# Seven block products for the second unit, with expert 0's weight sums made beside the first unit's outputs

## The chip, the core and the metric

The kernel runs on one core of one Trainium2 chip. The metric is the device time of one execution in microseconds (us). The engines are PE (TensorE matmul), ACT (ScalarE), DVE (VectorE), POOL (GpSimd) and SP (SyncE, which here only issues DMAs). Each engine works through its own instructions in order, and they meet only at semaphores.

## The reference

```python
h = layernorm(x) * (1 + ca) + sa                 # x: 4 x 2048 x 512
x = x + ga * attn(h)                             # rmsnorm, one 512 -> 1536 product, gated scan over time
h = layernorm(x) * (1 + cb) + sb
probs = softmax(h @ Wr); topk_probs, topk_experts = top_k(probs, 2)     # 8 experts
buf[e, b, pos] += h                              # at most 320 tokens per expert and batch row, the rest dropped
h1 = relu(buf @ W1 + b1)                         # 512 -> 2048
y  = h1 @ W2 + b2                                # 2048 -> 512
out = x + gb * sum over the 2 chosen experts of prob * y[token]
```

## The kernel before

The 8192 tokens are worked through in 16 blocks of 512 (four per batch row). An attention part runs over the blocks; each block is then normed, routed and its rows scattered by POOL into a table of slots in HBM (two times four indirect DMAs, line 710). The route of a block is route_choose (14 linked small DVE operations, line 1246), positions (a few small matmuls, line 1802) and route_place (up to 14 more links, line 1267). The last blocks, 14 and 15, are routed inside the first expert unit.

The expert part has 16 units, v = 0 to 15: expert e = v // 2 and half u = v % 2. A unit is 640 slots (two batch rows of 320). Every float32 factor is split into a high and a low float16 part, so each product is three matmuls. First layer: 512 to 2048 for 640 slots. Second layer: five column tiles of 128 slots, each 48 matmuls of 512 columns, in two PSUM banks by turns; column tile t needs the first operation of outputs(t - 2) (line 1446), which empties its bank.

Units below PLAIN (here 2) are plain: 16 column blocks hb of 24 matmuls of 320 columns, for two batch rows each. ACT and DVE follow in 32 steps i = 2 hb and 2 hb + 1: ACT makes the relu twice (float32 and float16) and DVE subtracts for the low part. Because b is the innermost loop, both steps of an hb end together. A step may be at most four ahead of the next engine's. Between the steps stand the last blocks' pieces, by hand: last_block(i) on DVE (line 1463) and ACT (line 906), last_block(hb) on PE (line 1864) behind the matmuls of hb, so that PE stands still there if its condition is not met. DVE also takes the maxima of w2 of expert 0 at steps 14, 16, 18 and 20, makes its scale at step 21 (w_scale, which goes over POOL's all_max) and the low parts (w_lo) at 25, 27, 29 and 31; ACT casts the high parts at 24, 26, 28 and 30.

Other units use seven block products in place of eight (Strassen's scheme in Winograd's form), 336 matmuls for 384, in a pipeline written out by slots: eight column pairs p, each started PERIOD = 7 slots after the one before, with pair_step(v, p, k) on PE, ACT and DVE for slot k = t - 7 p. They need sums of the four blocks of W1 (sums, line 1576, four linked DVE operations for each of two halves f, then ACT's casts sums_hi and DVE's rests sums_lo) and of the inputs (x_sums and x_lo, line 1597). For expert e + 1 this is made beside the outputs of unit (e, 1), after its weights were read once for their maxima (max_piece, line 1491) and loaded again.

Weights pass through four staging quarters q in reg_d. On SP, bring() waits until a quarter was released (s_rel[q], counted) and issues a 512 KB load (line 563), which counts s_fill[q]. fill_max, fill_w1 and fill_w2 give the number of loads ahead of a purpose. The order of SP's queue is that of experts() (line 591). Unit 1's input load (load_unit, a DMA transpose, line 538) waits for all scatters.

## Time and profile before

| | us |
|---|---|
| median of 3 runs | 2186.25 |
| lowest, highest | 2185.34, 2189.82 |
| profiled execution, its own time | 2185.74 |
| span of its profile | 2184.0 |
| PE busy | 2149.5 |
| DVE busy | 1602.7 |
| ACT busy | 1030.6 |

The span is what the profile shows from the first to the last instruction; times in rows are counted from its start. A PE matmul's busy time overlaps the next one's, so lengths of stretches are taken from starts. "Idle before" in a row is how long the engine stood still ahead of it, and the arrow names what released it.

### The profile page before, as it was taken

How to read it: one execution, taken by the hardware profiler on the slowest of the kernel's cores; microseconds unless marked ns; L12 is line 12 of the kernel's file. 1: busy time of each engine (PE TensorE's matmuls, PEld its weight loads, DVE VectorE, ACT ScalarE, POOL GpSimd, SP SyncE). 2: the span in 40 equal slices, each digit the busy share in tenths (PEclk: the TensorE clock that was granted, in tenths of full speed). 3: DMA queues.
4: the chain of work that ended last, by engine and by line, in shares of the span. 5: the costliest groups of instructions: out<-in, count | busy, mean ns of one | idle time of the engine just before them, and what ended most of it. 6: DMA issues, size and time to landing. Idle time of an engine off the chain costs nothing.

```text
span 2184.0 us, 33604 instructions
## 1 busy us (share of the span) xinstructions
PE 2149.5 (98%) x12538; PEld 1185.8 (54%) x12538; DVE 1602.7 (73%) x2850; ACT 1030.6 (47%) x2042; POOL 365.5 (17%) x334
## 2 busy tenths in 40 slices
PE   7999999999999999999999999999999999999997
PEld 2444454545564656556464655556464655656463
DVE  6799999999883587587668758775975887587341
ACT  5466666766370545246153625534461544356050
POOL 1124343343423010100101010110101010000101
PEclk9999999999999999999999999999999999999999
DMA  7799996775675344344534534452445345343301
GB/s 275 243 245 254 239 246 159 184 175 125 159 207 129 102 121 142 86 112 116 136 88 121 144 89 123 109 150 70 104 139 120 94 129 150 78 102 97 44 6 25
DMA packets 350883, 296.73 MB, mean 136 GB/s; under 512 B 242331, under 2 KB 242331, under 8 KB 350208
## 3 DMA queue, kind: packets, MB, share of 16 engines
q1 hardware_dynamic: 328960, 252.44, 41.5%
q0 software_dynamic: 21760, 42.14, 10.3%
q8 instruction: 99, 1.62, 0.3%
q14 instruction: 64, 0.52, 0.1%
HBM read 159.64 MB, written 93.01 MB: 116 GB/s over the span
## 4 chain that ended last, share of the span: by engine, by line
PE 90%; DVE 5%; SPq 1%; issue 1%; DMA 1%; ACT 1%; POOL 0%; DVEq 0%; ACTq 0%; POOLq 0%
PE bank L1979 36%; PE bank L1915 29%; PE bank L1831 20%; PE bank L1903 3%; PE bank L1786 1%; DMA reg_e<-reg_e 1%; SPq L491 0%; SPq L473 0%; PE bank L1742 0%; DVE reg_a L1568 0%; DVE reg_c L1179 0%; DVE reg_b L1438 0%; DVE mxw L1157 0%; DMA mod_rows<-reg_a 0%; PE bank L1797 0%
## 5 line engine op out<-in xcount | busy, mean ns | idle before, releaser
L1979 PE MATMUL bank<-reg_b,reg_c 128*128 128x512 f16 x3840 | 834.2, 379 | 1.2 <-DVE reg_b L1438 1.0
L1979 PEld LDWEIGHTS bank<-reg_b,reg_c 128*128 128x128 f16 x3840 | 375.3, 98 | 450.4 <-DVE reg_e L1456 2.1
L1831 PE MATMUL bank<-reg_c 128*128 128x512 f16 x2304 | 507.1, 379 | 1.5 <-DMA reg_c<-reg_a 1.4
L1915 PE MATMUL bank<-reg_e,reg_a 128*128 128x320 f16 x2688 | 417.7, 299 | 0.0
L1831 PEld LDWEIGHTS bank<-reg_c 128*128 128x128 f16 x2304 | 222.8, 98 | 260.7 <-issue 2.7
L1915 PEld LDWEIGHTS bank<-reg_e,reg_a 128*128 128x128 f16 x2688 | 262.2, 98 | 105.2
L736 POOL DMA_INDIRECT out_dram<-reg_e,midx x80 | 139.5, 1744 | 1007.2 <-DVE reg_e L1460 898.6
L1456 DVE SCALAR_TENSOR_TENSOR reg_e<-bank,inv,reg_e 128x512 f32<-128x512 f32 x80 | 59.8, 748 | 255.9 <-PE bank L1979 255.9
L947 ACT ACTIVATE reg_e<-bank,b1s 128x320 f32<-128x320 f32 x112 | 59.1, 527 | 390.4 <-PE bank L1915 390.4
L1915 PE MATMUL bank<-reg_e,reg_d 128*128 128x320 f16 x1344 | 217.0, 299 | 0.0
L1915 PEld LDWEIGHTS bank<-reg_e,reg_d 128*128 128x128 f16 x1344 | 130.4, 98 | 53.8 <-ACT reg_e L947 3.8
L689 POOL DMA_INDIRECT slot_rows<-reg_e,sli x112 | 129.2, 1154 | 100.7 <-DVE reg_e L1295 65.7
L1495 DVE TENSOR_REDUCE wm<-reg_d 128x1 f32<-128x1024 f32 x112 | 132.6, 1210 | 0.0
L1011 ACT ACTIVATE reg_e<-reg_e 128x2560 f16<-128x2560 f32 x14 | 32.7, 2337 | 194.3 <-DVE reg_e L1615 194.3
L1550 DVE SCALAR_TENSOR_TENSOR reg_e<-bank,reg_e 128x320 f32<-128x320 f32 x112 | 55.0, 491 | 85.3 <-PE bank L1915 84.2
L1915 PE MATMUL bank<-reg_e 128*128 128x320 f16 x672 | 109.6, 299 | 0.0
L1903 PE MATMUL bank<-reg_e,reg_a 128*128 128x320 f16 x768 | 105.9, 299 | 1.4 <-ACT reg_c L931 1.3
L856 ACT ACTIVATE reg_e<-bank,iq 128x512 f32<-128x512 f32 x60 | 40.9, 681 | 135.0 <-PE bank L1831 127.8
L1903 PEld LDWEIGHTS bank<-reg_e,reg_a 128*128 128x128 f16 x768 | 74.7, 98 | 31.3 <-ACT reg_c L931 2.3
L975 ACT ACTIVATE reg_c<-reg_e 128x320 f16<-128x320 f32 x112 | 52.1, 465 | 66.5 <-DVE reg_e L1550 66.5
L1568 DVE SCALAR_TENSOR_TENSOR reg_a<-reg_d,wsc,reg_a 128x1024 f16<-128x1024 f32 x56 | 69.4, 1281 | 16.8 <-ACT reg_a L989 16.8
L1915 PEld LDWEIGHTS bank<-reg_e 128*128 128x128 f16 x672 | 65.8, 98 | 27.8
(231 smaller groups left out, 2597.3 us busy)
## 6 DMA issues: line engine op xcount, KB each, us to landing
reg_d<-in_w SPq DMA_DIRECT2D x224, 512.0 KB, 4.1
slot_rows<-zrow SPq DMA_DIRECT2D x32, 516.0 KB, 5.1
reg_b<-in_x SPq DMA_DIRECT2D x16, 1024.0 KB, 7.6
out_dram<-reg_b SPq DMA_DIRECT2D x16, 1024.0 KB, 6.9
reg_d<-in_w SPq DMA_DIRECT2D x8, 1024.0 KB, 10.0
slot_rows<-zrow SPq DMA_DIRECT2D x32, 129.0 KB, 4.8
reg_d<-in_wmod SPq DMA_DIRECT2D x4, 1024.0 KB, 14.5
reg_e<-mod_rows SPq DMA_DIRECT2D x7, 512.0 KB, 4.1
```

The source lines that it names most:

```text
L689: g.indirect_dma_start(out=rows, out_offset=bass.IndirectOffsetOnAxis(ap=sli[:, pj % 2, k, t:t + 1], axis=0), in_=rowi[:, pj % 2, t, :], i ...
L736: g.indirect_dma_start(out=out, out_offset=bass.IndirectOffsetOnAxis(ap=midx[:, u, t:t + 1], axis=0), in_=yo[:, i % 2, :], in_offset=None, ...
L947: a.activation(part_of[:, n % 2, :], u_bank, ACT.Identity, bias=ba[:, p:p + 1], scale=HID_SHIFT).then_inc(s_r0, 1)
L975: a.activation(hid[:, 0, p, CAP:UNIT], part_of[:, 2 + n % 3, :], ACT.Relu).then_inc(s_h12, 1)
L1456: v_.scalar_tensor_tensor(yv[:, i % 2, :], bank_y[i % 2][:, :], inv2[:, u, kind:kind + 1], b2t, ALU.mult, ALU.add).then_inc(s_yd, 1)
L1495: v_.tensor_reduce(wm[:, which, k:k + 1], stage_q[:, q, :, :].rearrange("p c h -> p (c h)"), AX, ALU.max, apply_absolute_value=True).then_ ...
L1550: v_.scalar_tensor_tensor(part_of[:, 2 + n % 3, :], bank_v[n % 2][:, 0:CAP], HID_SHIFT, part_of[:, 2 + n % 3, :], ALU.mult, ALU.add).then_ ...
L1568: v_.scalar_tensor_tensor(lo, stage_q[:, q, :, :], wsc[:, 0:1], hi, ALU.mult, ALU.subtract).then_inc(s, 1)
L1831: ins = mm(dst[:, :], wqs[:, ws, kc, e0:e0 + P], xns[:, j % 2, xs, kc, :], start=kc == 0 and xs == 0 and ws == 0, stop=kc == KC - 1 and ws ...
L1903: ins = mm(bank_h[i % 4][:, 0:CAP], w1s[ws][:, kc, hb * P:(hb + 1) * P], xT_of(u)[:, 4 * xs + kc, b * CAP:(b + 1) * CAP], start=kc == 0 an ...
L1915: ins = mm(dst[:, 0:CAP], w[ws][:, c, p * P:(p + 1) * P], xs_of[:, KC * xs + 2 * i + c, j * CAP:(j + 1) * CAP], start=first and c == 0 and ...
L1979: ins = mm(bank_y[i % 2][:, :], hid[:, hs, hc, t * P:(t + 1) * P], w2s[:, ws, hc, :], start=k == 0 and hs == 0 and ws == 0, stop=k == HC - ...
```

## The change

PLAIN becomes 1: unit 1 has seven products too. For it, W1 of expert 0 is loaded again by quarters behind w_lo, in two halves (the second behind unit 1's input load on SP's queue), and DVE and ACT make its sums, their casts and rests, and the sums of unit 1's inputs, beside unit 0's outputs. Expert 1's first maxima for W1 move: four pieces to unit 0's outputs(3), four into the first four periods of unit 1, its scale_head to slot 30 and scale_tail to slot 51 there; the pieces for W2 stay in unit 1, eight, at slot 5 of each period. POOL's all_max(1, 0) moves in front of unit 1's outputs. In unit 0, block 15's norm (apply2, row_hi, lo2) moves ahead of block 14's routing, block 14's routing moves later (PE's logits from hb 2 to 4, positions from 5 to 6; DVE's route_choose from step 5 to 10, route_place from 9 to 14), and block 15's moves earlier (route_choose from 22 to 21, positions from hb 13 to 12, route_place from 28 to 25).

```diff
@@ constants
-PLAIN = 2
-W2_NEXT = 6
+PLAIN = 1
+W1_NEXT_HEAD, W1_NEXT_TAIL = 30, 51
@@ fill_max, fill_w1, fill_w2
-            return 8 * (e - 1) + 2 * which
+            return 8 * e - 6 + 2 * which
-            return 8 * (e - 1) + 4
+            return 8 * e - 2 if e else 0
-            return 8 * (e - 1) + 6
+            return 8 * e
@@ SP, experts()
-                bring_w1(1, fill_max(1, 0), 0)
+                bring_w1(0, fill_w1(0), 0)
                 for k in range(2):
                     sp.wait_ge(s_send[k], 16 * 2 * TB * NB // 2)
                 sp.wait_ge(s_xt, 16)
                 load_unit(1, 1)
+                bring_w1(0, fill_w1(0), 1)
+                bring_w1(1, fill_max(1, 0), 0)
@@ POOL
+                    if e == 0 and u == 1:
+                        all_max(1, 0)
-                        if e + 1 < E and u == 0 and t == (2 if e else 3):
+                        if 0 < e and e + 1 < E and u == 0 and t == 2:
@@ ACT, last_block(i)
+                if i in (7, 8):
+                    row_hi(n, 2 * (i - 7), 2 * (i - 7) + 2)
-                if i == 6:
+                if i == 12:
                     exps(n - 1)
-                if i in (10, 11):
-                    row_hi(n, 2 * (i - 10), 2 * (i - 10) + 2)
-                if i == 23:
+                if i == 22:
                     exps(n)
@@ ACT, sums_hi(e, f)
+                if e == 0:
+                    act.wait_ge(s_wlo, 8)
+                    act.wait_ge(s_mm1, 2 * HC)
                 for k, (w, q) in enumerate(((w_s1, 3), (w_s3, 2), (w_s2, 0), (w_s4, 1))):
-                    wait(act, s_ssum, 4 * (2 * (e - 1) + f) + k + 1)
+                    wait(act, s_ssum, 4 * (2 * e + f) + k + 1)
+                    if e == 0 and k == 3:
+                        for m in range(2):
+                            act.wait_ge(s_send[m], 16 * 2 * TB * NB // 2)
@@ ACT, behind unit 0
+                    if v == 0:
+                        sums_hi(0, 0)
                     if PLAIN <= v + 1 < 2 * E:
                         x_hi(v + 1)
+                    if v == 0:
+                        sums_hi(0, 1)
@@ DVE, last_block(i)
                 if i == 3:
                     apply2(q, j, 0)
-                if i == 5:
+                if i == 6:
+                    apply2(q, j, 1)
+                if i == 8:
+                    lo2(n, j)
+                if i == 10:
                     route_choose(q, j - 1)
-                if i == 7:
-                    apply2(q, j, 1)
-                if i == 9:
+                if i == 14:
                     route_place(q, j - 1)
-                if i == 11:
-                    lo2(n, j)
-                if i == 22:
+                if i == 21:
                     route_choose(q, j)
-                if i == 28:
+                if i == 25:
                     route_place(q, j)
@@ DVE, plain_unit(u)
-                    elif i >= W2_NEXT and i % 3 == 0 and (i - W2_NEXT) // 3 < 8:
-                        max_piece(1, 1, (i - W2_NEXT) // 3)
@@ DVE, pairs(v), u == 1
-                        if t % PERIOD == 2 and 1 <= t // PERIOD <= 8:
+                        if t % PERIOD == (2 if e else 5) and 1 <= t // PERIOD <= 8:
                             max_piece(e + 1, 1, t // PERIOD - 1)
+                        if e == 0 and t % PERIOD == 0 and 1 <= t // PERIOD <= 4:
+                            max_piece(1, 0, 3 + t // PERIOD)
+                        if e == 0 and t == W1_NEXT_HEAD:
+                            scale_head(1, 0)
+                        if e == 0 and t == W1_NEXT_TAIL:
+                            scale_tail(1, 0)
@@ DVE, beside_outputs(e, u, t), u == 0 and e == 0
                     if t == 0:
+                        sums(0, 0)
+                        sums_lo(0, 0)
+                    if t == 1:
+                        x_sums(1)
+                        sums(0, 1)
+                    if t == 2:
+                        x_lo(1)
+                        sums_lo(0, 1)
+                    if t == 3:
                         for k in range(4):
                             max_piece(1, 0, k)
-                    if t == 3:
-                        for k in range(4, 8):
-                            max_piece(1, 0, k)
-                        scale_head(1, 0)
-                    if t == 4:
-                        scale_tail(1, 0)
@@ PE, last_block(hb)
-                if hb == 2:
+                if hb == 4:
                     ... logits of block 14
-                if hb == 5:
+                if hb == 6:
                     positions(NB - 2, B - 1, BPB - 2)
-                if hb == 13:
+                if hb == 12:
                     positions(NB - 1, B - 1, BPB - 1)
@@ PE, pair_step, P1
-                    if p % 4 == 0 and v % 2 == 0:
+                    if p % 4 == 0 and (v % 2 == 0 or v == 1):
```

## Rows read from the trace of the kernel before

**Rows 1.** The page, part 1: busy us (share of the span) xinstructions.

```profile
PE 2149.5 (98%) x12538; PEld 1185.8 (54%) x12538; DVE 1602.7 (73%) x2850; ACT 1030.6 (47%) x2042; POOL 365.5 (17%) x334
```

**Rows 2.** Busy time by stretch: us, then PE, PEld, DVE, ACT, POOL, clock, DMA share.

```profile
589.50:648.30 58.80, 56.56 (x476) 40.97 (x475) 49.66 (x115) 38.91 (x82) 14.95 (x16) 1.00 0.75 194
701.50:753.70 52.20, 52.20 (x386) 37.57 (x384) 25.37 (x43) 26.83 (x61) 1.55 (x1) 1.00 0.29 86
753.70:805.50 51.80, 51.80 (x243) 23.49 (x241) 43.76 (x49) 19.45 (x19) 7.07 (x5) 1.00 0.50 111
805.50:903.00 97.50, 97.50 (x579) 56.21 (x577) 61.85 (x102) 38.98 (x73) 9.90 (x6) 1.00 0.48 125
```

**Rows 3.** Timeline of PE, end of unit 0: start, us, engine, operation, idle before.

```profile
629.43 0.25 PE L1797 MATMUL bank<-wrs,reg_e 128*128 128x16 f16 x4
...
630.23 9.94 PE L1903 MATMUL bank<-reg_e,reg_a 128*128 128x320 f16 x72
...
641.57 6.86 PE L1903 MATMUL bank<-reg_e,reg_a 128*128 128x320 f16 x47 [1.14 <-ACT reg_c L931]
648.27 5.34 PE L1979 MATMUL bank<-reg_b,reg_c 128*128 128x512 f16 x24
...
657.36 44.19 PE L1979 MATMUL bank<-reg_b,reg_c 128*128 128x512 f16 x204 [0.31 <-DVE reg_b L1438]
```

**Rows 4.** Timeline of DVE in unit 0.

```profile
596.80 0.49 DVE L1628 TENSOR_TENSOR reg_c<-reg_e,reg_c 128x320 f16<-128x320 f32 x1 [2.35 <-ACT reg_c L931]
...
605.82 0.18 DVE L1253 COPY lgs<-bank 128x32 f32<-128x32 f32 x1
...
608.73 0.19 DVE L1266 TENSOR_TENSOR mh<-oh 128x32 f16<-128x32 f32 x1
...
648.19 0.18 DVE L1273 TENSOR_TENSOR eqt<-bank,lim 128x32 f32<-128x32 f32 x1
...
651.81 2.35 DVE L1438 SCALAR_TENSOR_TENSOR reg_b<-reg_d,wsc,reg_b 128x2048 f16<-128x2048 f32 x1
...
654.88 2.34 DVE L1438 SCALAR_TENSOR_TENSOR reg_b<-reg_d,wsc,reg_b 128x2048 f16<-128x2048 f32 x1
```

**Rows 5.** Timeline of ACT in unit 0.

```profile
595.82 0.53 ACT L930 ACTIVATE reg_e<-bank,b1s 128x320 f32<-128x320 f32 x1 [8.50 <-PE bank L1786]
...
636.54 0.32 ACT L807 ACTIVATE prb<-dlg,ir 128x32 f32<-128x32 f32 x1 [1.21 <-DVE dlg L1256]
...
642.22 2.02 ACT L898 ACTIVATE reg_b<-reg_d,wsc 128x2048 f16<-128x2048 f32 x1
```

**Rows 6.** Timeline of POOL: scatter of block 15.

```profile
652.25 2.81 POOL L715 DMA_INDIRECT slot_rows<-reg_e,sli  x1 [18.05 <-DVE reg_e L1295]
655.36 2.71 POOL L715 DMA_INDIRECT slot_rows<-reg_e,sli  x1 [0.31 <-issue]
...
664.77 0.98 POOL L715 DMA_INDIRECT slot_rows<-reg_e,sli  x1 [0.30 <-issue]
```

**Rows 7.** Timeline of SP's queue: issue of unit 1's load.

```profile
666.89 6.79 SPq L538 DMA_TRANSPOSE reg_e<-slot_rows  x1
```

**Rows 8.** Line 563 on SP, 675.9 to 678: issues, time to landing.

```profile
L563 SPq DMA_DIRECT2D reg_d<-in_w x2: 578/696/813, 675.5 to 676.3; - x2
...
DMA to landing us min/median/max: 8.3/8.5/8.7
```

**Rows 9.** Tile reg_d, 700 to 760: last line, eight fills' time to landing.

```profile
DMA to landing us min/median/max: 3.3/3.5/5.2
```

**Rows 10.** Timeline of DVE in unit 3.

```profile
917.67 1.21 DVE L1495 TENSOR_REDUCE wm<-reg_d 128x1 f32<-128x1024 f32 x1
919.54 0.49 DVE L1550 SCALAR_TENSOR_TENSOR reg_e<-bank,reg_e 128x320 f32<-128x320 f32 x1 [0.66 <-PE bank L1915]
...
956.48 1.23 DVE L1583 TENSOR_TENSOR reg_d<-reg_d 128x1024 f32<-128x1024 f32 x1 [0.49 <-DVE reg_a L1568]
```

**Rows 11.** Timeline of PE in unit 3, second layer.

```profile
990.36 10.53 PE L1979 MATMUL bank<-reg_b,reg_c 128*128 128x512 f16 x48 [0.15 <-DVE reg_e L1456]
```

7 lines of the change are left out of this document (4 added, 3 removed).

## The prediction

> **What bounds the kernel now.** I read the page's busy shares first: PE is busy for 98% of the span [rows 1], so whatever adds or removes PE time near unit 1 moves the end, and idle time elsewhere only matters where PE comes to wait for it. Then the busy time by stretch [rows 2]: unit 0's first layer takes 58.8 us with 56.6 busy; unit 1 takes 52.2 for its first layer and 51.8 for its second, with PE never idle; unit 2, which has seven products, takes 97.5 in all, also without idle time. All stretches run at a granted clock of 1.00. Last come the timelines of PE, ACT, DVE, POOL and SP around unit 0, because the change takes work out of unit 1's PE stream and puts its preparation, and a new order, into unit 0. The waits PE has there now are small: 1.14 us on ACT, and in the second layer 36 matmuls take 9.1 us (648.27 to 657.36) where at the 44.19/204 = 0.217 us of the row after it they would take 7.8, so 1.3 us of waits [rows 3].
>
> **What it saves.** A plain unit has 16 x 24 = 384 matmuls of 320 columns, one with seven products 8 x 7 x 6 = 336. Units 1 and 2 differ in nothing else for PE: 52.2 + 51.8 - 97.5 = 6.5 us saved [rows 2]. One column block ("hb", 24 matmuls) of a plain unit is 52.2/16 = 3.26 us. If all the rest hid beside PE, this would be the result. So I go through what is moved.
>
> **Unit 0's first layer: the new order of block 14's and 15's routing.** PE calls positions() behind hb 6 for block 14, and waits there for the whole of route_choose, which DVE now starts at step 10 instead of 5. Steps 10 and 11 both end with hb 5. From then: ACT is free, and DVE's subtraction of step 10 starts 1.05 us later (596.80 against 595.82 for the first of ACT's two copies, and about 0.07 before it) [rows 4, 5]; it takes 0.41 (0.49 busy, 0.08 of it under the next), and route_choose 3.1 (605.82 to 608.73 + 0.19) [rows 4]. That is 4.6 us, but PE is there after 3.26: a wait of 1.3 us. Before, there were two hb blocks more between them.
> Block 15: DVE's chain now runs without a pause from step 14 to route_choose at step 21. From the end of hb 7: 1.05, route_place 3.05 (the one at 648.19 is released to POOL by 652.25, with 0.85 of start on POOL, so 3.2; block 14's has one link less), four maxima of 2048 columns at 2.2 (twice the 1.13 net of a max_piece of 1024), eight subtractions of 0.41 = 3.3, route_choose 3.1: 19.3 us [rows 4, 6, 10]. PE reaches positions() behind hb 12 after 5 x 3.26 + 0.8 (logits, 629.43 to 630.23 [rows 3]) = 17.1: a wait of 2.2. Before, route_place and lo2 of that chain lay ahead of step 14.
> The exponent chain w_scale (some 1.8 us, an estimate: five links at route_choose's 0.22 and 0.7 for POOL's part) now stands behind that route_choose. From its end PE needs 0.1 + 3.26 to reach hb 14, while ACT needs w_scale, one cast of w2 (2.0 busy, 1.9 net [rows 5]) and a pair of relus (0.8): 4.3 with the last semaphore, so about 0.9 of wait there, then 0.25 at hb 15, as each pair of steps costs ACT 1.64 + 1.9 against PE's 3.26. Waits of today that this replaces: 1.14 [rows 3] and about 0.5 unlabelled (641.57 + 47 matmuls ends before 648.27); the first comes from ACT's wait for the routing [rows 5]. Sum: 1.3 + 2.2 + 0.9 + 0.25 and 0.15 for each restart, minus 1.6, gives **+3.0 us**: the second layer starts at 651.3, not 648.27. In its first column tile PE waits for w_lo: the four end at 650.6, 653.7, 656.8 and 659.9 (route_place now stands ahead of the first; 2.26 each and one or two subtractions between), PE needs them at 651.3, 653.9, 656.5, 659.1: 0.9 of waits against 1.3 today. Net +2.6; column tile 3 can start at 651.3 + 0.9 + 3 x 10.36 = **683.3**. Bounds: 1.5 (both routing waits only half as long, from the 0.41 steps hiding in gaps) and 4.
>
> **Unit 0's second layer: the new sums.** Column tile 3 needs the first operation of outputs(1), and DVE has x_sums(1) and sums(0,1) ahead of that. sums(0,1) needs four fills; SP issues them behind unit 1's load, and this waits for all of block 15's scatter. route_place(15) follows the subtraction of step 25, and this ACT's relu behind its first cast of w2, so it runs from 645.1 to 648.3, where today's ends at 651.4: sooner by 3 us. But the scatter's eight issues on POOL are not of one length: those at 652.25 and 655.36 take 2.81 and 2.71, the last 0.98 [rows 6], and each starts inside a w_lo of DVE, an operation with two SBUF sources (651.81 and 654.88), and ends 0.85 to 0.9 after it [rows 4]. So with all four w_lo beside the scatter, four of its issues are long, not two: starts at 649.15, 651.8, 654.9, 657.95, then 661.0, and four short ones of 1.28 each (or slowed by the sums, from 662 on): the last ends at 665.9 to 666.9. Today it ends at 665.75 and SP goes on at 666.89 [rows 6, 7]. I take 667.5: **nothing of the 3 us arrives**.
> By the Trainium skill, "SBUF — State Buffer", section "Who interferes with whom", a DVE instruction with two SBUF inputs holds up only GpSimd work that reads SBUF, and it infers that descriptor generation is not held up; by that the scatter would be over by 660 and the wait below a third as long (rival B). The rows of POOL speak against it here.
> From 667.5: the load takes 6.8 of SP [rows 7], its small one 0.6, so the first fill goes out at 674.9. Today's four there, the first at 674.3 and the last at 676.3, landed up to 8.7 us after issue, at 685.0: 10.7 from first to last landing [rows 8]. Same here: 685.6. Then four sums of 1.26 (1.23 busy) [rows 10] and the 0.75 of outputs(1): 691.5. PE waits 691.5 - 683.3 = **8.2 us**. Lower bound: four fills at the 1.7 us each that they show when nothing else moves (8.8 after the first) and a send complete at 667.0: 5.9. Upper: 10, if the sums slow the scatter and are slowed by it. The first half, sums(0,0) from 662.3 and their rests until 672.1, is ready 0.1 before tile 2 wants it (672.9, with 0.75 for outputs(0)): nothing, though without room. ACT's new waits (s_wlo 8, s_mm1, s_send) have x_hi(1) and the other casts queued behind them, and these are later wanted than the fills. Tile 4 wants outputs(2) at 701.4; x_lo and four rests make it 700.8: nothing.
>
> **Unit 1's first layer: two maxima a period.** A period of seven products lasts 5.71 us (42 x 52.2/384 [rows 2]); DVE's seven operations in it at 0.41 and one max_piece at 1.13 net are 4.0, and 0.66 of the gap stands before L1550 [rows 10]. For four periods there are two. 1.13 more fits, but max_piece(1,1,k) waits for a fill that can only start when max_piece(1,0,4+k) has released the quarter, 5 slots before. Release to landing: 3.3/3.5/5.2 us [rows 9]. So one period is 1.24 + 3.5 + 0.06 + 1.13 + two subtractions 0.82 = 6.75: DVE falls back by 1.04 a period. C12 may be 1.75 us late (three products, 2.45, less its own 0.5 and the semaphores) before PE waits at P5. It is late by 1.0, 2.1 and, with the three links of scale_head at t = 30, 3.6 in the periods k = 0, 1, 2: waits 0.45 and 1.7, **2.15 us**. Bounds: 1.0 with landings of 3.3 and 4 with one of 5.2. all_max(1,0) moves on POOL in front of unit 1; nothing is queued behind it that is wanted before.
> **Unit 1's second layer.** Unit 3, the same work, has output 2 0.15 us late for PE [rows 11], so this chain has no room; the last max_piece now stands three slots later and delays C12 and all behind it by 0.6 to 1.0 us. **+0.8** (0.3 to 1.3).
>
> **Sum.** -6.5 + 2.6 + 8.2 + 2.15 + 0.8 = +7.25 us, from the profiled execution's 2185.74 (span 2184.0 and 1.7 around it), 0.5 below the median of the three runs, 2186.25. On the median: **2193.5 us**, 0.33% slower. About 0.2% (4.4 us) is what a measurement of this kernel can tell from no change.
>
> **The rivals.**
> A, all hidden: the waits I find are absorbed, by buffers that I miscounted, and today's 1.6 us of waits in the first layer go as well. 2186.25 - 6.5 - 1.6 = 2178.1. For it: unit 2 and unit 0's present order show hardly a wait. Against it: route_choose against one hb block is plain arithmetic on rows. 0.12.
> B, ends on the other side: not slower. The scatter keeps 1.28 a issue, is over at 659 and SP loads unit 1 at 660.2; the fills then wait only for the rests of the first half (671.0) and land alone by 679.9; outputs(1) at 685.8, a wait of 2.5 instead of 8.2: 2187.8. It decides when that wait is under 5.3 us, which needs the sends complete by about 664.5. For it: six of today's eight issues are short. Against: the long ones lie under w_lo. 0.20.
> C, the loop of fills in unit 1 is worse: landings of 5.0 us, as one of eight shows [rows 9], make a period 8.25, 2.5 over; three such add 4.5: 2198.0. Two loads a period share the engines, but seldom at once. 0.06.
> That seven products save nothing in unit 1 I give no chance of its own: unit 2 is the same code.
> The forecast itself has 0.62.
>
> **Chances and range.** The forecast's own bounds are -6.5 + 1.5 + 5.9 + 1.0 + 0.3 = +2.2 and +13, seldom all at one end: nine tenths of it is over 2190.6. Slower: 0.56 + 0.06 = 0.62; same: 0.06 and nearly all of B, 0.25; faster: A and a little, 0.13. The range takes in B and leaves out A and the far end: 2185 to 2199.
>
> **What would show it.** PE waits behind hb 6 and hb 12, on DVE's L1266-type link, of 1.3 and 2.2 us; four POOL issues over 2.6 us in the scatter of block 15; unit 1's load issued at about 667; one PE wait of 8 us ahead of unit 0's column tile 3, on outputs(1); in unit 1 two PE waits of 0.4 and 1.7 at P5 and DVE idle ahead of max_piece(1,1,0..3); unit 1 as a whole at 100.5 us. Wrong if the load goes out before 664 (B), or no wait shows behind hb 6 (then DVE or ACT has more room than I count).

## The result and the profile after

The changed kernel takes 2193.39 us in the median of 20 runs (lowest 2189.44), the kernel before 2186.4 beside it (20 runs, lowest 2184.81): a ratio of 1.0030, with a 95% interval of 1.0023 to 1.0037. It is 0.3% slower, as forecast (2193.5), and the forecast range holds it. One run of the changed kernel took 3237.11 us at a granted clock of 0.655, where all others have 0.99 or more, and is left out of the ratio.

The profiled execution is the fastest of those runs: 2189.44 us, span 2187.7. It has to be read as such. Unit 0 starts at 589.08 in it and at 589.53 in the kernel before, and from there to the end it takes 1600.36 us against 1596.21, 4.15 more. The medians differ by 7.0. I come back to the other 3 us.

First the page's busy shares of the changed kernel:

```profile
PE 2144.8 (98%) x12490; PEld 1180.4 (54%) x12490; DVE 1639.8 (75%) x2896; ACT 1044.0 (48%) x2051; POOL 375.8 (17%) x334
```

Then its busy time by stretch (PE, PEld, DVE, ACT, POOL, clock, DMA share); the stretches are unit 0's first layer, its second, unit 1's first, its second, and unit 2.

```profile
589.10:650.60 61.50, 56.63 (x475) 40.72 (x474) 49.35 (x127) 39.26 (x82) 16.57 (x17) 1.00 0.71 185
650.60:708.95 58.35, 53.87 (x243) 23.51 (x241) 47.47 (x44) 15.50 (x15) 21.07 (x11) 0.97 0.61 174
708.95:755.50 46.55, 45.07 (x332) 31.98 (x330) 36.98 (x74) 26.34 (x60) 3.42 (x3) 1.00 0.47 140
755.50:808.95 53.45, 52.76 (x248) 23.98 (x246) 46.50 (x54) 20.04 (x20) 7.08 (x5) 1.00 0.48 116
808.95:906.30 97.35, 97.35 (x576) 56.12 (x575) 61.91 (x102) 39.05 (x73) 9.90 (x6) 1.00 0.47 129
```

The 48 products fewer are there (12490 against 12538 in [rows 1]), and PE is busy 4.7 us less. Unit 1 takes 100.0 us instead of 104.0 [rows 2]. Unit 0 gives it back: its first layer takes 61.5 instead of 58.8, its second 58.35 instead of 53.1. And one number in the second row is new: the granted clock is 0.97. Which waits stand behind this is shown by the waits of PE, from unit 0 to the end (us in total, times, longest), and the timeline of PE in units 0 and 1:

```profile
PE bank L2001 <- DVE reg_e L1470: 4.6, 2, 3.9
PE bank L1828 <- DVE mh L1280: 3.2, 2, 2.0
PE bank L1937 <- DVE reg_e L1564: 1.5, 1, 1.5
```

```profile
616.84 0.19 PE L1828 MATMUL bank<-mh,upper 128*128 128x32 f16 x1 [1.19 <-DVE mh L1280]
639.48 0.19 PE L1828 MATMUL bank<-mh,upper 128*128 128x32 f16 x1 [1.97 <-DVE mh L1280]
...
643.93 6.86 PE L1925 MATMUL bank<-reg_e,reg_a 128*128 128x320 f16 x47 [0.76 <-ACT reg_c L935]
650.62 5.34 PE L2001 MATMUL bank<-reg_b,reg_c 128*128 128x512 f16 x24
...
659.31 23.54 PE L2001 MATMUL bank<-reg_b,reg_c 128*128 128x512 f16 x108 [0.32 <-DVE reg_b L1452]
686.74 22.37 PE L2001 MATMUL bank<-reg_b,reg_c 128*128 128x512 f16 x96 [3.89 <-DVE reg_e L1470]
...
735.11 0.99 PE L1937 MATMUL bank<-reg_e,reg_d 128*128 128x320 f16 x6 [1.48 <-DVE reg_e L1564]
...
798.60 10.53 PE L2001 MATMUL bank<-reg_b,reg_c 128*128 128x512 f16 x48 [0.69 <-DVE reg_e L1470]
```

Every wait stands where the forecast has one: behind hb 6 and hb 12 (L1828, on the last link of route_choose), at ACT's relu, ahead of column tile 3 (the row with 3.89), once at P5 of unit 1's pairs (the forecast has two there) and once at its output 2. Only the size of the one before tile 3 differs much: 3.9 instead of 8.2. These rows answer [rows 3, 11].

Why tile 3 waits: POOL's scatter of block 15, then SP's load of unit 1 (start, time that the issue takes), then DVE's work ahead of outputs(1).

```profile
648.39 2.48 POOL L717 DMA_INDIRECT slot_rows<-reg_e,sli  x1 [8.21 <-DVE reg_e L1309]
...
657.24 2.76 POOL L717 DMA_INDIRECT slot_rows<-reg_e,sli  x1 [0.30 <-issue]
660.31 0.97 POOL L717 DMA_INDIRECT slot_rows<-reg_e,sli  x1 [0.31 <-issue]
...
666.30 4.67 SPq L538 DMA_TRANSPOSE reg_e<-slot_rows  x1
...
673.29 2.83 DVE L1622 TENSOR_TENSOR reg_e<-reg_e 128x2560 f32<-128x2560 f16 x1 [0.24 <-DMA reg_e<-slot_rows]
...
681.02 1.23 DVE L1598 TENSOR_TENSOR reg_d<-reg_d 128x1024 f32<-128x1024 f32 x1 [1.46 <-DMA reg_d<-in_w]
```

The scatter starts 3.9 us sooner than in [rows 6], and the load goes out at 666.30, 0.6 before that of [rows 7]: four long issues instead of two (648.39 to 657.24) eat the gain up, as forecast. But the load then takes SP 4.67 us instead of 6.79, and the four fills behind it are used 9.4 us after the first of them is issued (671.63 to 681.02).

Of PE's 3.89 us only 1.70 are time in which DVE itself stands idle for a DMA: 0.24 ahead of the sums of x and 1.46 ahead of the second half's sums (the last two rows). DVE is busy for the rest, from its first sums at 661.81 on, with work that stands ahead of outputs(1). So an earlier load of x, or earlier fills behind it, could have taken 1.7 us off this wait and no more.

Last, what the forecast doesn't have at all, in three stretches of 4 us around the wait ahead of tile 3 (the clock is the number after POOL's):

```profile
682.00:686.00 4.00, 0.85 (x4) 0.20 (x2) 3.90 (x5) 3.45 (x3) 0.00 (x0) 1.00 0.00 0
686.00:690.00 4.00, 3.26 (x9) 1.22 (x10) 3.96 (x6) 1.15 (x1) 1.71 (x1) 0.57 0.00 0
690.00:694.00 4.00, 4.00 (x20) 1.82 (x19) 4.00 (x5) 0.00 (x0) 1.80 (x1) 1.00 0.44 49
```

Busy for 4.00 us at full clock, PE has 20 products in the last row; busy for 3.26 us behind the wait it has 9, at a mean granted clock of 0.57, nearly all of it at the lower level (1.2 GHz). The 96 products of tiles 3 and 4 take 22.37 us; at the 0.217 of [rows 3] they would take 20.8. So the wait costs 1.6 us again after it is over.

### The profile page after: what moved, and what is told of

The parts are those of the page before. It is cut to its first block, busy times and chain, and to the rows that moved or that the text cites. A ratio compares the mean times of both kernels' runs of the same rounds, so it can differ in the third digit from the quotient of the medians.

```text
span 2187.7 us, 33619 instructions
## 1 busy us (share of the span) xinstructions
PE 2144.8 (98%) x12490; PEld 1180.4 (54%) x12490; DVE 1639.8 (75%) x2896; ACT 1044.0 (48%) x2051; POOL 375.8 (17%) x334
## 4 chain that ended last, share of the span: by engine, by line
PE 86%; DVE 7%; DMA 2%; issue 2%; SPq 2%; POOL 1%; ACT 0%; DVEq 0%; POOLq 0%; ACTq 0%
PE bank L2001 33%; PE bank L1937 30%; PE bank L1853 20%; PE bank L1808 1%; DMA reg_d<-in_w 1%; DVE reg_a L1582 1%; PE bank L1925 1%; SPq L473 0%; POOL slot_rows L717 0%; DVE wmx L1393 0%; PE bank L1764 0%; DMA reg_d<-in_wmod 0%; DVE reg_e L1247 0%; DMA reg_e<-reg_e 0%; DVE reg_c L1193 0%
## 5 line engine op out<-in xcount | busy, mean ns | idle before, releaser
L1937 PE MATMUL bank<-reg_e,reg_a 128*128 128x320 f16 x2880 | 447.5, 299 | 0.0
L1937 PEld LDWEIGHTS bank<-reg_e,reg_a 128*128 128x128 f16 x2880 | 280.9, 98 | 112.7
L951 ACT ACTIVATE reg_e<-bank,b1s 128x320 f32<-128x320 f32 x120 | 63.3, 528 | 414.6 <-PE bank L1937 414.5
L1937 PE MATMUL bank<-reg_e,reg_d 128*128 128x320 f16 x1440 | 232.5, 299 | 1.5 <-DVE reg_e L1564 1.5
L1937 PEld LDWEIGHTS bank<-reg_e,reg_d 128*128 128x128 f16 x1440 | 139.5, 98 | 59.4 <-ACT reg_e L951 4.0
L691 POOL DMA_INDIRECT slot_rows<-reg_e,sli x112 | 129.7, 1158 | 100.3 <-DVE reg_e L1309 65.3
L1937 PE MATMUL bank<-reg_e 128*128 128x320 f16 x720 | 117.4, 299 | 0.0
L1937 PEld LDWEIGHTS bank<-reg_e 128*128 128x128 f16 x720 | 70.4, 98 | 29.7
L964 ACT ACTIVATE reg_e<-bank,b1s 128x320 f32<-128x320 f32 x120 | 63.4, 528 | 39.9 <-PE bank L1937 39.9
L1545 DVE SCALAR_TENSOR_TENSOR reg_c<-reg_e,reg_c 128x320 f16<-128x320 f32 x120 | 59.0, 492 | 30.4 <-ACT reg_c L960 28.9
```

Source lines behind the costliest of these rows:

```text
L691: g.indirect_dma_start(out=rows, out_offset=bass.IndirectOffsetOnAxis(ap=sli[:, pj % 2, k, t:t + 1], axis=0), in_=rowi[:, pj % 2, t, :], i ...
L951: a.activation(part_of[:, n % 2, :], u_bank, ACT.Identity, bias=ba[:, p:p + 1], scale=HID_SHIFT).then_inc(s_r0, 1)
L964: a.activation(part_of[:, 5 + n % 2, :], u_bank, ACT.Identity, bias=bb[:, NP + p:NP + p + 1], scale=HID_SHIFT).then_inc(s_r2c, 1)
L1545: v_.scalar_tensor_tensor(hid[:, 1, p, 0:CAP], part_of[:, n % 2, :], 0.0, hid[:, 0, p, 0:CAP], ALU.max, ALU.subtract).then_inc(s_l11, 1)
L1937: ins = mm(dst[:, 0:CAP], w[ws][:, c, p * P:(p + 1) * P], xs_of[:, KC * xs + 2 * i + c, j * CAP:(j + 1) * CAP], start=first and c == 0 and ...
```

## The experiments

For each run the timeline of PE gives the same marks, in us from the first product of unit 0 (that start itself lies at 589 to 596 us in these executions, in kernels that don't differ up to it). "To the end" is the profiled time minus that start. That start alone moves by 7.4 us from one execution to the next, which the medians hold and the marks don't. From unit 2 to the end every kernel takes 1380.0 to 1380.5 us, so all that differs lies ahead of it. Each row is one execution: the same first layer takes 61.5 us in five of them and 62.4 in e9. Ratios are to the kernel before on the same chip, whose median was 2187.1 beside the first four runs, 2187.6 beside the next four, 2190.6 beside three more and 2192.4 beside the last.

| kernel | layer 1 of unit 0 | layer 2 | unit 1 | unit 2 starts | to the end | ratio (95%) |
|---|---|---|---|---|---|---|
| before | 58.7 | 53.1 | 104.0 | 215.8 | 1596.2 | 1 |
| after | 61.5 | 58.3 | 100.0 | 219.9 | 1600.4 | 1.0030 (1.0023 to 1.0037) |
| e1 old order | 58.7 | 66.7 | 101.4 | 226.9 | 1607.3 | 1.0041 (1.0027 to 1.0055) |
| e2 only order | 61.5 | 52.7 | 104.0 | 218.2 | 1598.6 | 1.0013 (1.0004 to 1.0022) |
| e3 outputs first | 61.5 | 52.8 | 105.5 | 219.9 | 1600.3 | 1.0022 (1.0013 to 1.0031) |
| e4 maxima later | 61.5 | 59.9 | 99.2 | 220.6 | 1601.0 | 1.0033 (1.0021 to 1.0045) |
| e5 short w_lo | 61.5 | 57.1 | 100.1 | 218.7 | 1598.7 | 1.0012 (1.0002 to 1.0021) |
| e8 mixed order | 58.3 | 59.7 | 100.6 | 218.6 | 1599.0 | 1.0015 (1.0006 to 1.0024) |
| e6 mixed, outputs first | 58.3 | 52.8 | 106.1 | 217.2 | 1597.6 | 1.0011 (1.0002 to 1.0020) |
| e9 longer wait | 62.4 | 65.3 | 100.2 | 227.9 | 1608.0 | 1.0058 (1.0040 to 1.0076) |
| e10 before, mixed | 60.1 | 52.7 | 104.0 | 216.7 | 1597.1 | 1.0007 (0.9998 to 1.0016) |
| e7 all three | 61.0 | 53.2 | 107.9 | 222.1 | 1602.5 | 0.9998 (0.9986 to 1.0010) |
| e11 maxima spread | 63.0 | 54.3 | 104.6 | 221.9 | 1602.2 | 0.9999 (0.9987 to 1.0011) |
| e13 fills first | 60.7 | 62.2 | 102.2 | 225.1 | 1605.4 | 1.0029 (1.0017 to 1.0041) |

### What the new order costs, alone

e2 is the kernel before with the new order of blocks 14 and 15 in unit 0's first layer, and nothing else of the change.

```
 last_block of DVE                   ACT: row_hi at 7, 8; exps(n - 1) at 12; exps(n) at 22
-5 choose 14,  9 place 14            PE:  logits 14 at hb 4, positions 14 at hb 6,
-7 apply2, 11 lo2, 22 choose, 28 place    positions 15 at hb 12
+6 apply2, 8 lo2, 10 choose 14
+14 place 14, 21 choose, 25 place
```

> The kernel before with the new order of unit 0's first layer alone; unit 1 stays plain. Theory: 2.6 us slower than before (waits of 1.2 and 2.0 us at the two positions, 0.8 at hb 14, less 1.6 of today's), nothing given back, since nothing later waits for block 15's rows. Rival (the order costs nothing by itself, the waits come from the new work around it): within 0.5 us of before.

Measured: 2190.63 in the median, ratio 1.0013, and by the marks 2.3 us more than before: the +2.6 of the forecast. Its PE shows

```profile
PE bank L1806 <- DVE mh L1266: 3.2, 2, 2.0
```

at the positions, the same 1.19 and 1.97 as the changed kernel. So the order by itself is somewhat under half of the loss by the ratios (1.0013 of 1.0030), and it is paid without the seven products too.

e1 is the changed kernel with the old order put back.

> The change with the order of unit 0's first layer as it was before (logits, positions, route_choose, route_place, row_hi, exps at their old places); seven products in unit 1 stay. Theory (one chain by way of block 15's scatter, SP's load and the fills sets column tile 3): PE's waits behind hb 6 and hb 12 (1.2 and 2.0 us) go, the second layer starts some 2.5 us sooner, but route_place(15) ends 3 us later and the scatter not sooner, so the wait ahead of column tile 3 grows by as much: within 1 us of the changed kernel. Rival (the costs add up independently): 2.8 us less than the changed kernel. Second rival (the new order brings the load sooner, as it was meant to): slower by 3 us.

By the marks it takes 6.9 us more than the changed kernel. So the theory (within 1 us) fell, and the second rival came, slower because the new order brings the load sooner. The median, 2197.29, points the same way, but the ratios of the two differ by 0.0011 only and their intervals overlap.

```profile
673.09 10.53 PE L2001 MATMUL bank<-reg_b,reg_c 128*128 128x512 f16 x48 [0.68 <-DVE reg_e L1470]
...
693.18 23.84 PE L2001 MATMUL bank<-reg_b,reg_c 128*128 128x512 f16 x96 [9.56 <-DVE reg_e L1470]
```

The old order lets PE come to tile 3 some 2.8 us sooner, but unit 1's load goes out 1.2 us later (78.4 after unit 0's start, 77.2 in the changed kernel), and the fills, issued 1.5 later, are used 11.9 us after the first is issued instead of 9.4. The wait grows by what PE is early and the fills are late, and the clock is at 0.50 for longer behind it. So in the changed kernel the 2.8 us of the new order cost nothing by themselves, since PE has to wait ahead of tile 3 in any case, and the order brings the issue of the fills 1.5 us sooner. The other 2.5 us, from issue to use, aren't shown to come from the order: other kernels show 9.1 to 13.4 us there. My theory had judged it by the 0.6 us by which the load moved against the kernel before, and not by what the kernel with seven products and the old order would have.

e8 tells which part of the order pays. Block 14's steps go back, block 15's choice, placing and positions stay.

```
-DVE 6 apply2, 8 lo2, 10 choose 14, 14 place 14     ACT row_hi 7, 8; exps 14 at 12    PE hb 4, 6, 12
+DVE 5 choose 14, 7 apply2, 9 place 14, 11 lo2      ACT row_hi 10, 11; exps 14 at 6   PE hb 2, 5, 12
 DVE 21 choose 15, 25 place 15                      ACT exps 15 at 22
```

> The changed kernel, with block 14's steps in unit 0's first layer back at the places of the kernel before (apply 7, place 9, lo2 11, choose 5, row_hi 10 and 11, exps 6, logits hb 2, positions hb 5) and only block 15's choice, placing and positions at the new ones (21, 25, hb 12). Theory (the old order was slower by 3 to 4 us because block 15's placing came late there, and the new one pays 1.2 us for block 14's positions at hb 6): the wait of 1.2 at block 14's positions goes, the load is issued as in the changed kernel, about 77 us after the start of unit 0, tile 3 waits about 4: 2191.5 to 2193. Rival (block 15's norm has to come sooner, with row_hi at 7 and 8 and lo2 at 8, for its choice to be on time; the places of the choice alone bring nothing): a wait of 2 us or more ahead of block 15's positions or logits, load at 78 or later, tile 3 waits more than 6: 2195 to 2197 as in the old order.

```profile
640.59 0.18 PE L1828 MATMUL bank<-mh,upper 128*128 128x32 f16 x1
644.92 6.86 PE L1925 MATMUL bank<-reg_e,reg_a 128*128 128x320 f16 x47 [0.65 <-ACT reg_c L935]
...
667.42 4.80 SPq L538 DMA_TRANSPOSE reg_e<-slot_rows  x1
...
687.98 23.53 PE L2001 MATMUL bank<-reg_b,reg_c 128*128 128x512 f16 x96 [4.01 <-DVE reg_e L1470]
```

Not one wait is left at either positions, not only block 14's (e13, with the same order, has one of 0.73 us at block 15's): the second, 1.97 us, had also come from block 14's late steps in front of block 15's. The first layer takes 58.3 us, less than before, and the load goes out 74.1 us after unit 0's start instead of 77.2. Theory and rival both had the load at 77 us or later and missed that. It is 2190.66 in the median, below the theory's 2191.5 to 2193, and the ratio is 1.0015: about half of the loss is gone. (The wait ahead of tile 3 stays at 4.0, since PE is early by as much as the load, and the slow clock behind it takes 1.2 us more than in the changed kernel, so only 1.4 of the 3.3 us arrive by the marks.)

e10 is the kernel before with that same mixed order.

> The kernel before (unit 1 with nine products), with block 15's choice, placing and positions alone at their new places (VectorE 21 and 25, TensorE hb 12, exps at 22) and block 14 left where it was. Theory (the 2.3 us that the change's whole order costs in the kernel before come from block 14's later steps and the waits that they cause; block 15's part costs nothing): no wait ahead of either positions, first layer of unit 0 in 58.3 us against 58.74, the whole at most 0.5 below the kernel before: ratio 0.9995 to 1.0000. Rival (block 15's sooner placing pushes VectorE's remainders and the second layer's w_lo): waits of 1 us or more at the second layer's start, ratio 1.0005 to 1.001.

Neither quite. No wait at the positions, but the first layer takes 60.1 instead of 58.3, 1.2 of it a stall ahead of the logits for which the profile has no releaser; e7 and e13 show one of that size too and e11 one in three parts (0.19, 0.49, 0.56), while e6 and e8, with the same order on another chip, don't. The ratio 1.0007 (0.9998 to 1.0016) can't be told from no change. What that stall is stays open.

### What makes tile 3 wait

e5 shortens the operations of DVE that lie beside the scatter.

```
-v_.scalar_tensor_tensor(lo, stage[:, c, :], wsc[:, 1:2], hi, ALU.mult, ALU.subtract)
+v_.tensor_scalar(lo, stage[:, c, :], wsc[:, 1:2], None, ALU.mult)   # w2 of expert 0 only
```

It leaves out the subtraction of the high part, so the low part is not the remainder; the number of products is the same.

> The changed kernel, with the four low parts of expert 0's second weights (w_lo, 2.35 us each on VectorE, two SBUF sources) made by one tensor_scalar with a single SBUF source. Left out: the high part is no longer subtracted, so w2's low part of expert 0 is not the remainder; the number of products is the same. Disputed: what lengthens four of the eight issues of block 15's scatter on GpSimd (2.48 to 2.76 us instead of 0.97). Theory (an operation of VectorE with two sources in SBUF holds GpSimd's issues back): all eight issues take about 1 us, the scatter is over by some 6.5 us sooner from the start of unit 0, SyncE's transposing load of the block's x is issued about 6 us sooner (71 instead of 77.2 us after the start of unit 0), and the wait of 3.9 us ahead of unit 0's column tile 3 goes or falls below 1, with the slow clock behind it: 3 to 5.5 us less than the changed kernel, 2188 to 2190. Rival (it is VectorE's share of the SBUF as such, or the weights' traffic, whatever the operation's form): the four issues stay at 2.5 or more and the time within 1 us of 2193. Second rival (the issues get short, but the load isn't what the wait hangs on: the fills of the stage buffers are): issues short, load sooner, the wait of tile 3 still above 2.5 us.

```profile
650.05 1.60 POOL L717 DMA_INDIRECT slot_rows<-reg_e,sli  x1 [8.20 <-DVE reg_e L1309]
...
655.90 0.97 POOL L717 DMA_INDIRECT slot_rows<-reg_e,sli  x1 [0.30 <-issue]
657.18 1.61 POOL L717 DMA_INDIRECT slot_rows<-reg_e,sli  x1 [0.30 <-issue]
...
649.47 1.29 DVE L1456 TENSOR_SCALAR reg_b<-reg_d,wsc 128x2048 f16<-128x2048 f32 x1 [0.30 <-DVE reg_e L1309]
...
663.78 4.77 SPq L538 DMA_TRANSPOSE reg_e<-slot_rows  x1
...
671.66 1.28 DVE L1588 SCALAR_TENSOR_TENSOR reg_e<-reg_d,wsc,reg_e 128x1024 f16<-128x1024 f32 x1
...
686.96 22.58 PE L2007 MATMUL bank<-reg_b,reg_c 128*128 128x512 f16 x96 [2.77 <-DVE reg_e L1476]
```

Both halves of it teach something. DVE's operations take 1.28 us instead of 2.35, and still four of POOL's issues are long, 1.6 to 1.7, one under each (the fourth, with none of DVE's beside it, takes 0.97): the first ends at 651.65, 0.89 after DVE's first (650.76), where in the changed kernel the first ends at 650.87, 0.91 after its w_lo (647.61 + 2.35). So the theory's mechanism holds (DVE holds the issue until its own operation is over), but not its reason: one SBUF source is enough. Second, the load goes out 4.2 us sooner by the marks, and the wait falls by 1.1 only. The fills can't follow: the first goes out at 671.76, when the third of the first sums' remainders has freed its buffer (the row at 671.66 is the fourth; the third ends at 671.74). That is what the second rival said, and it is rival B of the forecast, whose working gave a wait of 2.5 us. But DVE is idle for only 0.68 us ahead of these sums, where it was idle for 1.70 in the changed kernel: what is left of the wait, 2.1 us, is DVE's own work from its first sums on. The ratio is 1.0012, down from 1.0030.

e9 makes the wait longer.

```
 sums(0, 1)
+dve.wait_ge(s_ssum, 8)
+for k in range(2):
+    v_.tensor_reduce(mxw[:, k:k + 1], stage[:, 0, :], AX, ALU.max, apply_absolute_value=True)
```

> The changed kernel, with two reductions of 128x2048 elements (some 4.5 us of VectorE together, values not used) put ahead of unit 0's outputs(1), so that the wait of TensorE ahead of tile 3 gets longer on purpose. Theory (the wait is paid one for one, and the clock behind it stays at 1.2 GHz for longer, as in the run with the old order: 96 products in 23.8 behind 9.6 us of wait against 22.4 behind 3.9): wait 8 to 9, 96 products in 23.4 to 24, and 4.5 + 1.2 us over the changed kernel, 2198 to 2200. Rival (the wait at tile 3 is slack that a later wait takes up, in the fill loop of unit 1): the fill loop's wait of 1.48 shrinks or goes, and the time is at most 2 us over the changed kernel, 2195.5.

```profile
698.12 23.46 PE L2004 MATMUL bank<-reg_b,reg_c 128*128 128x512 f16 x96 [9.05 <-DVE reg_e L1470]
```

and its busy time by stretch around that:

```profile
689.00:693.00 4.00, 0.07 (x1) 0.00 (x0) 3.86 (x5) 3.52 (x4) 0.00 (x0) 1.00 0.00 0
693.00:698.00 5.00, 0.00 (x0) 0.00 (x0) 5.00 (x3) 1.07 (x1) 0.00 (x0) 0.51 0.00 0
698.00:703.30 5.30, 5.18 (x13) 1.88 (x14) 5.26 (x7) 0.00 (x0) 3.51 (x1) 0.50 0.00 0
703.30:708.00 4.70, 4.70 (x23) 2.12 (x22) 4.63 (x5) 0.00 (x0) 0.00 (x0) 0.99 0.77 143
```

The theory holds: 2199.8 in the median of four runs, 6.4 over the changed kernel, and the 1.48 of unit 1's fill loop is unchanged (1.5), so no later wait takes up what is added ahead of tile 3. PE sits idle for 4 us at full clock, then the clock is granted at 0.50, and is still at 0.50 in the 5.3 us in which products run again: 13 products in 5.18 us against 23 in 4.70. The cost of it doesn't follow the length of the wait: 96 products take 22.6 us behind a wait of 2.8 (e5), 22.4 behind 3.9 (after) and 5.8 (e13), 23.4 to 23.5 behind 3.7 (e4), 4.0 (e8) and 9.0 (e9), 23.8 behind 9.6 (e1), and 20.8 would be full speed: 1.6 to 3.0 us.

e3 takes the wait away by the order of DVE's work: outputs 1 to 3 of unit 0 go ahead of the sums, remainders and maxima beside them.

```
-beside_outputs(e, u, t); outputs(e, u, t)
+outputs(e, u, t); beside_outputs(e, u, t)      # for unit 0, t = 1, 2, 3
```

> The changed kernel with DVE's outputs(1), outputs(2) and outputs(3) of unit 0 ahead of the sums, casts' rests and maxima that stand before them. Theory: the wait ahead of column tile 3 (3.9 us in the profile) and the slow clock behind it (about 1.5 us) go; DVE then reaches unit 1 with its four maxima waiting for fills until 706 us, up to 3 us after PE: 2185.5 to 2189, 4 to 8 us under the changed kernel, with a new wait of 1 to 3 us at the start of unit 1. Rival (that wait is not what costs the time, the DMA engines are, and the work moves with them): no more than 1.5 us gained.

```profile
664.38 44.28 PE L2005 MATMUL bank<-reg_b,reg_c 128*128 128x512 f16 x204 [0.32 <-DVE reg_b L1452]
715.94 0.99 PE L1941 MATMUL bank<-reg_e,reg_a 128*128 128x320 f16 x6 [2.33 <-DVE reg_e L1541]
726.37 0.99 PE L1941 MATMUL bank<-reg_e,reg_d 128*128 128x320 f16 x6 [2.00 <-DVE reg_e L1564]
```

By the marks the 204 products run in one piece at full clock, as before [rows 3]. Then unit 1's first layer waits for 6.3 us (2.33, 2.00 and two more, 0.49 and 1.52) where it waited for 1.5, and unit 2 starts at 219.9, as in the changed kernel. The rival's size came: the median, 2192.64, is 0.8 us lower, which is inside the error. The marks fit a chain of fill, sum, remainder, next fill, maximum, next fill, that runs through both units and sets the time whichever of its users stands first on DVE. What is taken away at one end of it, wait and slow clock together (5.5 us), comes back at the other (5.5).

e6 puts the mixed order and the outputs first together.

> As the run with the mixed order, and outputs 1 to 3 of unit 0 ahead of the sums, remainders and maxima made beside them. If each part gives what it gave alone (outputs first: 0.5 to 1 less than the changed kernel, block 14 in its old place: about 1 less): 2191 to 2192, no slow clock in unit 0's second layer, but 2 us of wait at unit 1's start and up to 2 in its fill loop. Rival (waits are set by the chain that runs from block 15's scatter through the load, the fills and the sums, whatever the order of PE's feeders): as the run with outputs first, within 0.5 of 2192.6.

2191.14, ratio 1.0011, within the theory's 2191 to 2192. By the marks it is the best of the kernels with seven products (unit 2 at 217.2): both parts are there, 3.3 us less in the first layer and no slow clock, and unit 1 waits 6.9 us for the chain, 4.3 of them in its fill loop where the theory had up to 2. The ratios can't tell it from e3 or e8.

e13 tries to start that chain sooner: the four fills go ahead of the wait for the scatter and of the load. DVE's and ACT's work beside unit 0's outputs is put in another order to follow it, which the lines below leave out; so the run doesn't tell these parts from one another.

```
 bring_w1(0, fill_w1(0), 0)
+bring_w1(0, fill_w1(0), 1)
 for k in range(2): sp.wait_ge(s_send[k], ...)
 load_unit(1, 1)
-bring_w1(0, fill_w1(0), 1)
```

> The changed kernel with the mixed order (block 14 at its old places) and one more part moved: SyncE issues the four fills for the second half of expert 0's sums ahead of its wait for block 15's scatter and the transposing load, not behind them, and the work beside unit 0's outputs follows that: the second four sums, output 1, their remainders, output 2, the sums of x, output 3, two maxima, x's low part, two maxima, output 4; ScalarE casts the second sums before x. Theory (the wait ahead of tile 3 comes from five operations of x_sums, 5.9 us, and a queue in which the fills stand behind a load that needs the whole scatter): the fills are issued 1 us sooner and without a load beside them, the sums are over by 683 minus nothing of x_sums, the wait ahead of tile 3 falls from 4.0 below 1, no clock of 1.2 GHz behind it, the remainders free their buffers 5 us sooner, so the maxima don't wait: unit 2 starts 212 to 214.5 us after unit 0 (218.6 with the mixed order alone, 215.8 before), ratio to the kernel before 0.998 to 1.000. Rival (the fills can't start sooner, since the first sums' remainders free their buffers only at 671, and x gets late instead): tile 3 waits 2 to 3 and unit 1's start another 2 to 3: unit 2 at 217 to 219, ratio 1.001 to 1.002.

A miss, and worse than the rival too: ratio 1.0029, and unit 2 at 225.1.

```profile
678.75 16.85 SPq L538 DMA_TRANSPOSE reg_e<-slot_rows  x1
...
688.57 1.22 DVE L1598 TENSOR_TENSOR reg_d<-reg_d 128x1024 f32<-128x1024 f32 x1 [9.90 <-DMA reg_d<-in_w]
...
694.29 22.41 PE L2005 MATMUL bank<-reg_b,reg_c 128*128 128x512 f16 x96 [5.82 <-DVE reg_e L1470]
```

Behind four fills the transposing load takes SP 16.85 us, not 4.7, and lands 20.0 after its issue, where it landed 7.0 after in the changed kernel. The fills gain nothing: the first goes out at 676.1, when its buffer is free, and the sums start at 688.6, 12.5 us later. In e8, with the same order of blocks and the load ahead, it is 9.4 us. So the load is slowed by standing behind the fills. That it slows them is not shown, since 12.5 us lies within the 9.1 to 13.4 of the kernels with the load ahead.

### The fill loop of unit 1

e4 makes unit 1's eight maxima of w2 one period later, so that a fill has a period and two slots to land instead of five slots.

```
-if t % PERIOD == (2 if e else 5) and 1 <= t // PERIOD <= 8: max_piece(e + 1, 1, t // PERIOD - 1)
+if e == 0 and t % PERIOD == 2 and 2 <= t // PERIOD <= 9:    max_piece(1, 1, t // PERIOD - 2)     # e > 0 as before
```

> The changed kernel with the eight maxima of w2 in unit 1 one period later and at slot 2 (t = 16, 23 ... 65 for 12, 19 ... 61), so that each has nine slots instead of five since the release that its fill waits for. Theory (a loop of release, fill and maximum of 6.3 to 6.75 us against a period of 5.71): DVE waits for no fill, PE's 1.5 us wait at P5 goes, the last maximum comes 4 slots later and adds 0.5 to the wait in unit 1's second layer: 1 us less. Rival (DVE has simply too much to do with two maxima a period): the wait stays at 1 us or more, no gain.

The wait at P5 is gone altogether, as the theory says, and unit 1's first layer runs without a pause in 44.9 us instead of 46.55. The second layer gives half of it back:

```profile
802.07 10.53 PE L2003 MATMUL bank<-reg_b,reg_c 128*128 128x512 f16 x48 [1.53 <-DVE reg_e L1470]
```

1.53 us ahead of output 2 instead of 0.69, since all later fills come later. Its median is no better (1.0033). Up to unit 1 its trace is the changed kernel once more, in a more usual execution (2192.80). There unit 0's second layer takes 59.9 us instead of 58.3, with a wait of 0.5 us ahead of output 0 and 2.6 us of slow clock instead of 1.6. The wait ahead of tile 3 is 3.7, much as in the changed kernel's own trace.

e7 has the three parts together, the mixed order, the outputs first and the maxima later; e11 has also output 4 ahead of the maxima and these spread over the gaps.

> The changed kernel with three parts moved: the mixed order (block 14 at its old places), outputs 1 to 3 of unit 0 ahead of the sums, remainders and maxima, and unit 1's eight maxima of w2 one period later. Theory (each wait has its own cause and they add): the waits of 4.3 in unit 1's fill loop that the kernel without the later maxima has go, the wait of 2.6 at unit 1's start stays, 3 to 4 us less than that kernel's 2191.1: 2187 to 2188. Rival (the maxima later only move the wait, as they did alone: by one period later fills come later and unit 1's outputs wait): 2190.5 to 2191.5, with waits of 1.5 or more in unit 1's second layer.

> As the run with the three parts moved, and beside that output 4 of unit 0 goes ahead of the maxima too: of the four maxima made after output 3, the first stays, the second comes after output 4, and the third and fourth in unit 1's first period (slots 1 and 5). Theory (the wait of 2.6 at unit 1's start is VectorE's outputs 3 and 4 standing behind four maxima that wait for their fills): that wait falls below 1, 2 us less than the run with the three parts moved: 2185 to 2187, at or below the kernel before. Rival (the fills are late by themselves, and the fourth maximum in the loop holds C11 and C22 of the first pair up as before): the wait moves to the first products of the pairs, no more than 0.5 gained.

Their ratios are 0.9998 and 0.9999, with intervals that reach from 0.9986 to 1.0011: not told from the kernel before, and 0.3% below the changed one. The medians are less kind, 2191.96 and 2192.71 against 2190.55, and the marks contradict them: from unit 0's start to the end both profiled executions take 6 us more than the kernel before. These two executions are among the slowest of their runs (2196.11 of 2186.73 to 2196.19 for e7), so neither trace shows where a fast one saves.

e7's trace has something of both sides. No wait is left in unit 1's fill loop, as its theory says, but the wait at unit 1's start is 3.7 instead of 2.6, and its second layer has the rival's wait of over 1.5:

```profile
635.95 8.35 PE L1931 MATMUL bank<-reg_e,reg_a 128*128 128x320 f16 x48
...
803.72 12.22 PE L2007 MATMUL bank<-reg_b,reg_c 128*128 128x512 f16 x48 [2.01 <-DVE reg_e L1470]
```

The clock is slow behind three of its stalls: behind the one of 1.2 us ahead of block 15's logits (48 products in 8.35 us, 6.68 at full clock), behind the 3.7, and behind the 2.0 (48 in 12.22, 10.53 at full clock). e11 doesn't differ from e7 in time, and its rival came: its first wait of unit 1 fell from 3.68 to 0.32 as meant, and PE then waits at the next products instead.

```profile
715.47 0.99 PE L1944 MATMUL bank<-reg_e,reg_a 128*128 128x320 f16 x6 [0.32 <-DVE reg_e L1541]
721.99 1.57 PE L1944 MATMUL bank<-reg_e,reg_a 128*128 128x320 f16 x6 [2.17 <-ACT reg_e L956]
```

No kernel tried is shown to beat the one before. With seven products in unit 1 these two come so close to it that the runs can't tell them apart.

## Why the prediction was right, point by point

**The saving.** Forecast -6.5. Unit 1 takes 100.0 us, with 2.2 of waits; without them 97.85, against 103.96 before: 6.1. Forecast for the unit as a whole: 100.5.

**The order.** Forecast: waits of 1.3, 2.2 and 0.9, and the second layer 3.0 later. Measured: 1.19, 1.97, 0.76, and 2.8. Alone (e2), it costs 2.3, forecast 2.6. The step is right in place and size. (Its parts add to 3.05 before the 0.15 for each restart, so as written the sum is somewhat over its 3.0.) What e8 adds is that both waits come from block 14's late steps; I had worked the second from the whole chain of DVE, of which they are a part.

**The wait ahead of tile 3.** Forecast 8.2, measured 3.9 in the profiled execution: this is the term that was mis-sized. Its first half is right: four long issues instead of two (2.48 to 2.76), the load at 666.3 (forecast 667.5, with unit 0 starting 0.45 sooner). The second half took two durations from [rows 7, 8]. The load's issue took 4.67 instead of 6.79, and fills were used 9.4 us after the first was issued instead of 10.7; together with the 0.75 of the load that makes the sums start 4.2 us sooner from unit 0's start, and the wait shorter by as much.

The first of these was an odd value in its own trace: the kernel before issues such a load 15 times, in 4.65 us at least, 4.94 in the median and 6.79 at most, and the forecast took the 6.79. Nor is it mere chance. Unit 1's load takes 6.55 to 7.14 in the three kernels with a plain unit 1 (before, e2, e10) and 4.67 to 5.03 in all ten with seven products and the load ahead; why is not shown. The second does vary: 9.1 to 13.4 us pass from the first fill's issue to the sums (9.1 in e4, 9.4 in after and e8, 9.5 in e5, 10.8 to 11.2 in e3, e6, e7 and e9, 11.9 in e1, 13.4 in e11). The forecast's 10.7 lies in that spread, and its lower bound of 5.9 for the wait didn't allow for the shorter issue.

**The slow clock.** Not in the forecast: 1.6 us in the profiled execution, up to 3.0 in others. The waits of up to 2.0 us at the positions show none here (clock 1.00 in the first layer), but e9's do.

**The loop and the second layer.** Forecast 2.15 and 0.8, measured 1.48 (one wait, not two) and 0.69. DVE does idle ahead of all of the first four maxima of w2, 1.49, 1.02, 1.33 and 0.79 us. e4, in which PE no longer waits there once each maximum has four slots more, shows that the time a fill gets is the cause.

**The sum.** By the profiled executions: +4.15 instead of +7.25, with tile 3's term 4.3 too large, the loop's 0.7 too large, the saving 0.4 too large and the clock's 1.6 missing. By the medians: +7.0. e4's unit 0 is a second sample of the same instructions, and is 1.5 us longer: 1.05 by the clock behind tile 3's wait and 0.4 ahead of output 0. Its wait ahead of tile 3 is 3.7 us, so the 8.2 is twice too large for a usual execution too. Where the rest of the 7.0 lies is not shown by any trace of a median run. The later landings of fills are one candidate, and what comes before unit 0 (589.1 to 596.5) is another. So the mechanism was right in all but the clock, and that the median came out at 2193.4 was luck in part: a term 4.3 us too large stood in for the slow clock, which the forecast left out, and for about 3 us that the traces don't place.

**The rivals.** A (all hidden) didn't come; of the waits that the forecast found only one of the two at P5 was absent. B's premise was false for the kernel (the issues are long), but e5 made it nearly true, and there B's working held: the fills wait for the remainders, and the wait is 2.8 (worked out: 2.5), most of it with DVE busy. C (three landings of 5 us in the loop) didn't come: nine fills there land in 3.2 us at least, 3.6 in the median and 7.6 at most, and PE waits once.

## What to carry to other kernels

Where a change fills idle stretches of one engine, follow the buffers and not only the engine's time: here each stage buffer goes round from fill to sum to remainder to the next fill, and a wait taken away at one place came back at the next one. Take durations of a DMA from several executions, and look for the same DMA elsewhere in the trace: 14 more loads stood in this one, and most took 4.9 us where the forecast took 6.8. Give the term their whole spread, split a wait into DMA time and work of the engine waited for, and allow for a slow clock behind each longer wait of TensorE. And try the parts of a reordering one by one, since the part that pays (block 15's steps sooner) and the part that costs (block 14's later) came in one edit.
